# Projecting the queries of a retention block chunk by chunk instead of pair by pair of heads

## What is computed

```python
h = layernorm(x) * (1 + ca) + sa
q = rotary(h @ Wq.T);  k = rotary(h @ Wk.T)      # 8 heads x 64
v = h @ Wv.T;          g = h @ Wg.T              # 8 heads x 128
scores = (q @ k.T) * D ** -0.5 * decay           # causal, for each head
o = groupnorm(scores @ v) * silu(g)
x = x + ga * (o @ Wo.T)
h = layernorm(x) * (1 + cb) + sb
x = x + gb * ffn(h)                              # sigmoid(r) * (relu(k)**2 @ Wv)
```

## Time and profile before

| | |
|---|---|
| time, median of 3 runs | 769.07 us (768.91 to 770.2) |
| span of the profiled execution, first to last instruction | 764.9 us |
| what lies around the span, by the median | 4.2 us |
| busy in the span: TensorE products / loads | 736.1 us (96%) / 648.9 us (85%) |
| busy: VectorE / GpSimd / ScalarE | 623.1 (81%) / 587.1 (77%) / 452.3 us (59%) |
| mean granted clock of TensorE | 0.990 |

### The profile page before, as it was taken

The page is one execution under the profiler, slowest core; times in us unless marked ns, Lnnn a source line. Parts: engine busy times, 40 slices in busy tenths (PEclk is TensorE's granted clock), DMA queues, the critical chain, the costliest instruction groups (busy, mean ns, idle before and its releaser), DMA issues.

```text
span 764.9 us, 29122 instructions
## 1 busy us (share of the span) xinstructions
PE 736.1 (96%) x12121; PEld 648.9 (85%) x12121; DVE 623.1 (81%) x1326; ACT 452.3 (59%) x819; POOL 587.1 (77%) x641
## 2 busy tenths in 40 slices
PE   5788999999999999999999999999999999999996
PEld 4566888898988988889898889889888888988875
DVE  6988787988879887888979888797888888787545
ACT  4244546666575566656556565655656565656664
POOL 2757777887878888797878977788887978777651
PEclk9899999999999999999999999999999999999998
DMA  9422221122123122222312212231321222122100
GB/s 326 126 43 44 44 43 39 29 43 53 29 44 71 32 62 43 44 51 43 72 27 67 43 40 56 43 70 24 71 43 36 60 43 55 25 59 43 38 15 28
DMA packets 65235, 41.41 MB, mean 54 GB/s; under 512 B 38096, under 2 KB 54736, under 8 KB 65104
## 3 DMA queue, kind: packets, MB, share of 16 engines
q1 hardware_dynamic: 64384, 38.75, 21.8%
q10 hardware_dynamic: 720, 0.80, 0.3%
HBM read 10.17 MB, written 4.19 MB: 19 GB/s over the span
## 4 chain that ended last, share of the span: by engine, by line
PE 91%; DVE 4%; issue 1%; ACT 1%; DMA 1%; POOL 1%; SPq 0%; ACTq 0%; DVEq 0%; POOLq 0%
PE ring L275 51%; PE outs L275 14%; PE O_E L275 14%; PE ring L290 7%; PE O_O L275 3%; PE ring L314 2%; DMA consts<-in_const 1%; DVE N L922 1%; DVE swapped L871 1%; POOL gn_rstd L1150 0%; DVE turned L866 0%; DVE gn_sum L915 0%; POOL y L1157 0%; DVE h_full L851 0%; DMA k_odd<-rot_k 0%
## 5 line engine op out<-in xcount | busy, mean ns | idle before, releaser
L1157 POOL TENSOR_TENSOR y<-y,gate 128x512 f32<-128x512 f32 x123 | 155.1, 1284 | 27.3 <-ACT y L628 27.3
L1140 POOL TENSOR_TENSOR rot_k<-rot_k,sin_k 128x256 f32<-128x256 f32 x128 | 108.6, 870 | 35.5 <-DVE sin_k L888 35.5
L275 PEld LDWEIGHTS outs<-wo_gated,y 128*128 128x128 f32 x992 | 127.2, 191 | 9.6 <-POOL y L1157 1.7
L275 PE MATMUL outs<-wo_gated,y 128*128 128x128 f32 x992 | 131.3, 275 | 1.1 <-POOL y L1157 1.0
L915 DVE TENSOR_REDUCE gn_sum<-N 128x4 f32<-128x512 f32 x128 | 81.8, 680 | 42.4 <-ACT N L616 42.4
L1150 POOL TENSOR_TENSOR gn_rstd<-gn_var,minus_half 128x8 f32<-128x8 f32 x64 | 105.4, 1646 | 5.0
L1134 POOL TENSOR_TENSOR qT<-qT,swapped 128x512 f32<-128x512 f32 x64 | 83.1, 1299 | 19.6 <-DVE swapped L871 19.4
L628 ACT ACTIVATE y<-ring,gn 128x512 f32<-128x512 f32 x126 | 90.9, 777 | 4.8 <-PE ring L290 4.8
L597 ACT ACTIVATE v_odd<-ring 128x512 f32<-128x512 f32 x64 | 38.3, 599 | 93.0 <-PE ring L275 93.0
L895 DVE TENSOR_TENSOR A<-ring,consts 128x256 f32<-128x256 f32 x128 | 47.9, 416 | 40.0 <-PE ring L275 40.0
L909 DVE TENSOR_TENSOR S<-ring,S 128x512 f32<-128x512 f32 x112 | 76.8, 686 | 1.9
(11 more groups left out here) (150 smaller groups left out, 2122.9 us busy)
## 6 DMA issues: line engine op xcount, KB each, us to landing
v<-v_odd SPq DMA_DIRECT2D x128, 128.0 KB, 2.3
k_odd<-rot_k SPq DMA_DIRECT2D x128, 64.0 KB, 2.2
X<-in_x SPq DMA_DIRECT2D x16, 256.0 KB, 3.3
out<-X SPq DMA_DIRECT2D x15, 256.0 KB, 3.1
key_tables<-in_const SPq DMA_DIRECT2D x7, 256.0 KB, 8.2
rotary_q<-in_const_q SPq DMA_DIRECT2D x2, 512.0 KB, 8.7
N<-in_w_qkT SPq DMA_DIRECT2D x1, 512.0 KB, 5.0
N<-in_w_vT SPq DMA_DIRECT2D x1, 512.0 KB, 6.2
```

The lines of the kernel that those rows point to most:

```text
L275: return e.matmul(o, lhsT, rhs, start=start, stop=stop, skip_group_check=True)
L1140: done = e.tensor_tensor(turned[:, n, :, :], turned[:, n, :, :], sin[:, n, :, :], op)
L1157: e.tensor_tensor(y[:, n % NY, :], y[:, n % NY, :], gate[:, n % 2, :], ALU.mult).then_inc(sem["y"])
```

## The change

Queries are projected for one chunk and all four pairs at a time: `project_q(i)` fills a bank with 4 x 128 columns, with twelve products whose moving operand is 128 tokens, where `project_q(m)` had three with 512. `rotate_q(i)` reads the tables of the chunk's 128 tokens once for all pairs (a broadcast), with as many elements an instruction as before. `qT` holds three chunks instead of two groups. The call for chunk i falls into step i - 1 on TensorE and VectorE (before: call m in step m - 4). Scores of chunk i wait for `qT` of that chunk alone. The norm of group 1 moves later: statistics from step -4 to 0, `full_h` and the transposes from -1 to 1; the low part of the value weights is made in step -1 instead of -4.

```diff
-NX, NHT, NQ, NN, NY, NS = 7, 4, 2, 2 * GC, 4, 3
+NX, NHT, NQ, NN, NY, NS = 7, 4, 3, 2 * GC, 4, 3
...
-        qT = sb("qT", [P, NQ, PAIRS, W])
+        qT = sb("qT", [P, NQ, PAIRS, P])
...
-            def project_q(m):
-                g, p = divmod(m, PAIRS)
-                cols = slice(p * P, (p + 1) * P)
-                bank = take_bank(("q", m), ("cos_q", m + 1))
+            def project_q(i):
+                g, j = divmod(i, GC)
+                h_chunk = h_parts(g, slice(j * P, (j + 1) * P))
+                bank = take_bank(("q", i), ("cos_q", i + 1))
                 at.wait_ge("w_qk_lo", 1)
                 at.wait_ge("hT_hi", g + 1)
                 at.wait_ge("hT_lo", g + 1)
-                split_matmul(bank[:, :], [wqk[s][:, cols] for s in ("hi", "lo")], h_parts(g)).then_inc(sem["proj_q"])
+                for n in range(PAIRS):
+                    pair = slice(n * P, (n + 1) * P)
+                    done = split_matmul(bank[:, pair], [wqk[s][:, pair] for s in ("hi", "lo")], h_chunk)
+                done.then_inc(sem["proj_q"])
...
             def scores(i):
-                at.wait_ge("qT", PAIRS * (i // GC + 1))
+                at.wait_ge("qT", i + 1)
...
-                for m in due(step + 4, 1, NCHUNK):
-                    project_q(m)
+                for i in due(step + 1, 1, NCHUNK):
+                    project_q(i)
...
-            def rotate_q(m):
-                g, p = divmod(m, PAIRS)
-                tokens = slice((g % GB) * W, (g % GB + 1) * W)
-                bank = bank_of["q", m]
+            def rotate_q(i):
+                c, bank = i % CB, by(PAIRS, bank_of["q", i][:, :])
+                cos, sin = (rotary_q[:, n, c * P:(c + 1) * P].unsqueeze(1).broadcast_to([P, PAIRS, P]) for n in range(2))
...
-                e.tensor_tensor(turned[:, :], bank[:, :], rotary_q[:, 1, tokens], ALU.mult).then_inc(sem["sin_q"])
-                at.wait_ge("o", GC * (g - NQ + 1))
-                e.tensor_tensor(qT[:, g % NQ, p, :], bank[:, :], rotary_q[:, 0, tokens], ALU.mult).then_inc(sem["cos_q"])
+                e.tensor_tensor(by(PAIRS, turned[:, :]), bank, sin, ALU.mult).then_inc(sem["sin_q"])
+                at.wait_ge("o", i - NQ + 1)
+                e.tensor_tensor(qT[:, i % NQ, :, :], bank, cos, ALU.mult).then_inc(sem["cos_q"])
...
+                for _ in due(step + 1, 1, 1):
+                    split_w("w_v", raw_vc, wv)
+                for i in due(step, 1, 2):
+                    norm_stats(i + 1, 0)
+                for g in due(step + 8, GC, NGROUP, 3):
                     norm_stats(g, 0)
...
-                for m in due(step + 4, 1, NCHUNK):
-                    rotate_q(m)
+                for i in due(step + 1, 1, NCHUNK):
+                    rotate_q(i)
...
-                for _ in due(step + 4, 1, 1):
-                    split_w("w_v", raw_vc, wv)
-                for g in due(step + 5, GC, NGROUP, 1):
+                for _ in due(step - 1, 1, 1):
+                    full_h(1)
+                for g in due(step + 5, GC, NGROUP, 2):
                     full_h(g)
```

More of the change, by code:

```diff
@@ L368, in queries @@
             def queries(i, odd, n, half):
-                g, j = divmod(i, GC)
-                return qT[halves(odd), g % NQ, n, j * P + half * HALF:j * P + (half + 1) * HALF]
+                return qT[halves(odd), i % NQ, n, halves(half)]
             def scores(i):
-                at.wait_ge("qT", PAIRS * (i // GC + 1))
+                at.wait_ge("qT", i + 1)
                 at.wait_ge("kT", i + 1)
@@ L536, in _ @@
                     mod_gates(0)
-                for g in due(step + 5, GC, NGROUP):
+                for _ in due(step + 5, 1, 1):
+                    transpose_n(0, 0)
+                for _ in due(step - 1, 1, 1):
+                    transpose_n(1, 0)
+                for g in due(step + 5, GC, NGROUP, 2):
                     transpose_n(g, 0)
@@ L746, in _ @@
                     norm_apply(g, 1)
-                for g in due(step + 7, GC, NGROUP, 1):
+                for _ in due(step + 1, 1, 1):
+                    norm_apply(1, 0)
+                for g in due(step + 7, GC, NGROUP, 2):
                     norm_apply(g, 0)
-                for g in due(step + 6, GC, NGROUP, 1):
+                for _ in due(step, 1, 1):
+                    round_h(1)
+                for g in due(step + 6, GC, NGROUP, 2):
                     round_h(g)
@@ L857, in low_h @@
                                 ).then_inc(sem["hT_lo"])
-            def rotate_q(m):
-                g, p = divmod(m, PAIRS)
-                tokens = slice((g % GB) * W, (g % GB + 1) * W)
-                bank = bank_of["q", m]
-                at.wait_ge("const_q%d" % (g % GB), 16)
-                at.wait_ge("proj_q", m + 1)
-                at.wait_ge("swapped", m)
-                e.tensor_tensor(turned[:, :], bank[:, :], rotary_q[:, 1, tokens], ALU.mult).then_inc(sem["sin_q"])
-                at.wait_ge("o", GC * (g - NQ + 1))
-                e.tensor_tensor(qT[:, g % NQ, p, :], bank[:, :], rotary_q[:, 0, tokens], ALU.mult).then_inc(sem["cos_q"])
-                at.wait_ge("sin_q", m + 1)
-                at.wait_ge("qT", m)
+            def rotate_q(i):
+                c, bank = i % CB, by(PAIRS, bank_of["q", i][:, :])
+                cos, sin = (rotary_q[:, n, c * P:(c + 1) * P].unsqueeze(1).broadcast_to([P, PAIRS, P]) for n in range(2))
+                at.wait_ge("const_q%d" % (c // GC), 16)
+                at.wait_ge("proj_q", i + 1)
+                at.wait_ge("swapped", i)
+                e.tensor_tensor(by(PAIRS, turned[:, :]), bank, sin, ALU.mult).then_inc(sem["sin_q"])
+                at.wait_ge("o", i - NQ + 1)
+                e.tensor_tensor(qT[:, i % NQ, :, :], bank, cos, ALU.mult).then_inc(sem["cos_q"])
+                at.wait_ge("sin_q", i + 1)
+                at.wait_ge("qT", i)
                 e.stream_shuffle(swapped[:, :], turned[:, :], PARTNERS).then_inc(sem["swapped"])
@@ L1033, in _ @@
                     ffn_weights(b)
-                for g in due(step + 8, GC, NGROUP, 1):
+                for _ in due(step + 1, 1, 1):
+                    split_w("w_v", raw_vc, wv)
+                for i in due(step, 1, 2):
+                    norm_stats(i + 1, 0)
+                for g in due(step + 8, GC, NGROUP, 3):
                     norm_stats(g, 0)
@@ L1128, in gate_weights, with rotate_q @@
                                 gates[:, b % 2, 0:C].unsqueeze(1).broadcast_to([P, PAIRS, C]), ALU.mult).then_inc(sem["wo_gated"])
[L1130 to L1134, removed]
+            def rotate_q(i):
+                q = qT[:, i % NQ, :, :]
+                at.wait_ge("swapped", i + 1)
+                e.tensor_tensor(q, q, by(PAIRS, swapped[:, :]), ALU.add).then_inc(sem["qT"])
             def rotate_k(i):
@@ L1199, in _ @@
                     ffn_out(g)
-                for m in due(step + 6, 1, NCHUNK):
-                    rotate_q(m)
+                for i in due(step + 3, 1, NCHUNK):
+                    rotate_q(i)
                 for _ in due(step - 2, 1, 1):
                     gate_weights(0, 0)
-                for g in due(step + 7, GC, NGROUP, 1):
+                for _ in due(step + 1, 1, 1):
+                    low_h(1)
+                for g in due(step + 7, GC, NGROUP, 2):
                     low_h(g)
@@ L1219, in _ @@
                     gate_weights(b, 0)
-                for g in due(step + 11, GC, NGROUP, 1):
+                for _ in due(step + 3, 1, 1):
+                    norm_rstd(1, 0)
+                for _ in due(step + 1, 1, 1):
+                    norm_rstd(2, 0)
+                for g in due(step + 11, GC, NGROUP, 3):
                     norm_rstd(g, 0)
```

## The result

The changed kernel takes 810.71 us (median of 4 runs, 810.38 to 811.26), and the kernel before, in the same job, 768.99. The ratio is 1.055, 95% interval [1.053, 1.057]: 5.5% slower, +41.7 us, where +37.7 was forecast.

A forecast was written before the change was run, and what follows sets the result against it. The prediction took PE (TensorE) to bound the kernel from step 5 on. Query products +38.5 us less 0.8 at the start gave +37.7, so 769.07 became 806.8, or 807 us, with a range of 768 to 813 us.

The forecast's parts named there:

- What bounds the kernel: From step 5 on, a microsecond added to or taken from PE's list is a microsecond of the kernel.
- The price of a narrow product: Query products of 128 columns on PE: 0.111 us each, twelve cost 1.33 us, 0.63 us more a step; chance 0.62.
- three bounds: Narrow query product on PE: 0.059 us by columns, 0.11 by its load, 0.222 by the nearest float32 product.
- The columns' price: Narrow query products on PE: loads hidden, twelve cost 0.705 us, total 770.4 us, no measurable change; chance 0.11.
- the case halfway: Narrow query products on PE: 0.085 us each, a call 1.02 us, +19.6 us, total 789 us; chance 0.08.
- The float32 price: Narrow query products on PE: 0.222 us each, 2.66 a call, total 885 us; chance 0.17.
- How many calls count: Query calls in steps 5 and later are paid in full: 55 x 0.705 before, 58 x 1.33 after, +38.5 us.
- VectorE with broadcast tables: Query rotation on VectorE: reading broadcast tables changes no time; 0.1 us an instruction would be covered by spare time.
- The new wait at nothing: Scores waiting for their own chunk's queries cost nothing; without cover 0.1 to 0.6 us a step, up to 35 us.
- The start: First steps: first state 3.4 us earlier, less later costs, gives 0.8 us back; bounds 3.4 gained and 1.5 lost.
- a keys' transfer lands 2.2 us after its issue: At the start, this transfer time lets the first state start near 24.0 us instead of 27.4.
- elsewhere in steps 0 to 4 the longer call lies in PE's 2.4 us to spare: Early steps on PE: longer query calls fit into 2.4 us of spare time in 10, so they add nothing.

The follow-up runs named there:

- q128: The kernel before with only its three query products of 512 columns cut into twelve of 128, old schedule kept: 804.5 us, ratio 1.048.
- q256: The kernel before with only its query products cut into six of 256 columns a call: 769.11 us, ratio 1.001.
- q64: The kernel before with only its query products cut into twenty-four of 64 columns a call: 919.3 us, ratio 1.198.
- lead2: The changed kernel with queries projected and rotated two chunks ahead of their scores instead of one, four buffers: 811.06 us, ratio 1.054.
- late_after2: The changed kernel with loads of key tables 3 to 7 and x 3 to 6 issued behind the first chunk's transfers, second run: 803.58 us, ratio 1.047.
- heads_first: The kernel before with VectorE rotating queries behind the head norm instead of ahead of it in steps 1 to 4: 773.47 us, ratio 1.007.

## Why the prediction was right

**What bounds the kernel: right.** PE stays full from 80 us on, and the 58 steps from 5 to 63 give +38.0 us for a forecast of +38.5.

**The price of a narrow product: right.** Forecast 0.111 us, measured 0.112 in the changed kernel and in q128. Of the three bounds the load's holds. The columns' price, by which nothing would change, is out by q128, and with it the case halfway. The 81 ns of the Trainium skill (TensorE: Matmul & The Clock Gate, Back-to-back issue gap) do not agree with these traces: streams of a full load and a narrow product run at 0.112 us here. The prediction's "no stream of that form is in this trace" was too narrow: the eight float32 records of the earlier trace rows have 128 columns and a load each, and are 0.111 us apart. The float32 price (0.222) is out too. q256 and q64 show that it is a floor under the columns' price and no property of 128 columns.

**How many calls count: right.** q128 has the old 55 calls in steps 5 to 59 and loses 34.6 us there, and the changed kernel has 58 and loses 38.0. The difference, 3.4 us, is near the 3 x 1.33 = 4.0 of the three calls in the last steps. Four steps take 47.1 us, as forecast.

**VectorE with broadcast tables: right.** 1326 records before and after, 623.1 and 630.2 us busy. The 7 us more are not the broadcast's: q128, without it, has 630.7. The rotation's two products take 683 and 681 ns in the mean with the broadcast table, 679 and 680 before.

**The new wait at nothing: right**, by lead2 and by PE's full stretches.

**The start: wrong, and it is the term that was mis-sized.** I forecast 0.8 us gained, with 1.5 lost as the far bound, which the listed terms do not even give (3.4 - 1.3 - 2.0 is 0.1 gained). The traces show 5.9 us lost by step 5, and the medians 41.7 - 38.0 = 3.7 us. The step that failed is "a keys' transfer lands 2.2 us after its issue", a duration taken from a later step and used where the queue was still full. Issued at 20.8 and 21.5, it landed shortly before 26.9. In the changed kernel's chain it is one piece, 5.1 us for the forecast's 2.2:

```profile
21.50 5.13 DMA k_odd<-rot_k
```

The gain of 3.4 us shrank to 0.5. Behind the wait the clock was at its lower level until 35.6 us (before: 30.2), and a query call there took 2.6 us in place of 1.33. Without these loads ahead (late_after2), the first state starts at 22.8 and the start is 2.1 us ahead of the kernel before, between the 0.8 and the 3.4 that I had reasoned; that this comes so near is in part luck, as no term of the sum stood for the clock. The error of the prediction is 4.0 us of 41.7: 4.5 too little for the start, less 0.5 too much for the full steps. Also, "elsewhere in steps 0 to 4 the longer call lies in PE's 2.4 us to spare" was too kind: in q128, which has the old schedule, step 5 comes 4.3 us late (77.97), 2.7 of it already at step 0 (30.45 against 27.72); its TensorE first reached the upper level at 27.5 us, 10.9 us later than in the kernel before.

## What to carry to other kernels

Where TensorE was full, a float32r product of 128 or 64 columns with a full load cost 0.112 us and one of 256 columns 0.117: below that width count the instructions, not the columns. Before work is moved to the front, look at the queue of transfers there: a transfer that took 2.2 us in a later step took 5.1 behind the loads of the start, and the engine that arrived early only waited longer, and went on at its lower clock. An order that frees an engine's chain may hold a PSUM bank longer, as heads_first suggests; follow the bank as well as the data.

## What the hardware showed that I had not expected

In q64 TensorE's granted clock was 0.94 to 0.97 in long stretches in which PE was recorded busy all the time; with 128 columns it was 1.00 in such stretches. Within them it changed between 1.00 and 0.50, with no idle time of PE ahead of the fall at 354 or at 395 us. Of the 132.9 us that q64 lost from step 5 to 63, 109 are the narrow products, and the other 24 go with the 54.6 us at the lower level, whose cost is estimated at up to 27.3 us. Why the clock fell there, and not with 128 columns, stays open.
